# Self-attention of a two-layer decoder: the rows of shifts issued by ACT instead of SP

## The reference

```python
# layer 0: 16 heads of 16, weights are signs times a row mean
q, k, v = split_heads(...)            # B, H, T, Dh
att = softmax(einsum('bhtd,bhsd->bhts', q, k) * scale)
y = einsum('bhts,bhsd->bhtd', att, v)
# layer 1: the same with a mask: 4 heads causal, 12 heads causal within a window of 64
scores = where(mask, -inf, scores)
```

## Time and profile before

| | us |
|---|---|
| median of 3 runs (2166.31 to 2177.34) | 2174.9 |
| the profiled execution | 2166.33 |
| its span, first to last instruction | 2164.6 |

### The profile page before, as it was taken

How to read it: one execution, slowest core, us unless ns; L and a number is a source line. 1 busy time by engine, 2 the same in 40 slices (tenths; PEclk the granted TensorE clock), 3 DMA queues, 4 the chain that set the end, 5 groups by cost and what they waited for, 6 DMA issues and landing times. The chain is left out here.

```text
span 2164.6 us, 35976 instructions
## 1 busy us (share of the span) xinstructions
PE 1685.7 (78%) x12334; PEld 860.6 (40%) x12350; DVE 1328.2 (61%) x3655; ACT 1111.9 (51%) x1526; POOL 929.9 (43%) x955
## 2 busy tenths in 40 slices
PE   4888888888687885577777775677658788999992
PEld 2222222222255563233333333344334455666661
DVE  2767777775177995356666663445267774555554
ACT  2367676765365894245555543355344443444440
POOL 3145455531458522367777764345223341222220
PEclk9899999997698998679999977889879999999996
DMA  4342233320130000334333301422123232222217
GB/s 101 64 70 55 56 49 63 57 45 2 43 83 1 1 1 11 62 58 58 57 56 52 51 11 25 95 52 52 26 90 120 103 132 67 61 62 62 61 49 245
DMA packets 120452, 130.26 MB, mean 60 GB/s; under 512 B 21981, under 2 KB 106973, under 8 KB 120125
## 3 DMA queue, kind: packets, MB, share of 16 engines
q1 hardware_dynamic: 109572, 105.54, 24.0%
q0 software_dynamic: 6480, 18.23, 2.2%
q10 hardware_dynamic: 4224, 4.19, 0.6%
HBM read 79.25 MB, written 47.55 MB: 59 GB/s over the span
## 5 line engine op out<-in xcount | busy, mean ns | idle before, releaser
L653 ACT ACTIVATE at_pexp<-ps 128x1024 f32<-128x1024 f32 (+3 forms) x480 | 385.7, 826 | 185.5 <-PE ps L890 184.5
L714 DVE TENSOR_REDUCE at_mx<-ps 128x1 f32<-128x512 f32 x512 | 323.7, 683 | 137.3 <-PE ps L897 135.5
L897 PE MATMUL ps<-at_ks,at_qs 48*128 48x512 f16 (+3 forms) x1024 | 284.5, 353 | 98.4 <-DVE at_mx L714 41.7
L161 PE MATMUL ps<-mo_wall,mo_xt 128*128 x1704 | 301.8, 327 | 0.9 <-issue 0.9
L890 PE MATMUL ps<-at_qs,at_ks 50*128 50x512 f16 (+4 forms) x1024 | 251.8, 345 | 20.5 <-DMA at_qs<-at_mhl 14.5
L950 PE MATMUL ps<-at_pexp,at_vaug 128*32 128x512 f32 (+4 forms) x2048 | 223.1, 528 | 12.0 <-issue 11.8
L161 PEld LDWEIGHTS ps<-mo_wall,mo_xt 128*128 128x128 f16 x1704 | 161.2, 98 | 94.7 <-issue 4.0
L2258 POOL DMA_INDIRECT mo_yd<-mo_xn,mo_idu x71 | 68.2, 960 | 272.1 <-DVE mo_xn L2520 263.0
L716 DVE CUSTOM_DVE_ANT_0 at_junk<-ps,at_lmask 128x192 bf16<-128x192 f32 x384 | 115.6, 352 | 81.8 <-PE ps L897 80.5
L897 PEld LDWEIGHTS ps<-at_ks,at_qs 48*128 48x128 f16 x1024 | 75.8, 97 | 210.5 <-DVE at_mx L714 121.4
L2311 ACT ACTIVATE mo_sg<-ps 128x512 f32<-128x512 f32 x71 | 42.4, 597 | 194.8 <-PE ps L161 194.8
(11 more groups left out here) (399 smaller groups left out, 3754.8 us busy)
## 6 DMA issues: line engine op xcount, KB each, us to landing
at_qs<-at_scratch SPq DMA_DIRECT2D x96, 128.0 KB, 7.1
at_ks<-at_scratch SPq DMA_DIRECT2D x96, 128.0 KB, 7.7
mo_xr<-mo_xs SPq DMA_DIRECT2D x71, 136.0 KB, 2.4
at_scratch<-at_qkh SPq DMA_DIRECT2D x64, 128.0 KB, 1.8
at_scratch<-at_qkl SPq DMA_DIRECT2D x64, 128.0 KB, 1.8
x_qs<-x_queries SPq DMA_DIRECT2D x48, 128.0 KB
mo_stage<-in_m_gate SPq DMA_DIRECT2D x9, 512.0 KB
mo_stage<-in_m_up SPq DMA_DIRECT2D x9, 512.0 KB
```

What stands on the lines that cost most here:

```text
L161: last = nc.tensor.matmul(out, lhs, rhs, start=(n == 0), stop=(n == len(terms) - 1))
L653: last = act.activation(columns(pexp[:, U % 2, hh], at, n, stride, width), columns(banks(r, ST[S % 2], 2), at, n, stride, width), ACT.Exp, ...
L714: last = ve.reduce_max(out, score, AX.X)
L897: return nc.tensor.matmul(banks(r, MX[i % 2])[:, piece.at:piece.at + piece.n], qs[rows, (n // 2) % 2, h // 2, piece.idx * P:(piece.idx + 1 ...
```

## The change

The function `rows` moves, with its wait and its four transfers, from SP's program to ACT's. ACT calls it in the step MT, right behind `turned_max`. The wait is on the semaphore that ACT's own copy counts up. Sizes, places, semaphores and all other programs stay.

```diff
-            def rows(n):
-                b, half = n // 2, n % 2
-                sp.wait_ge(mhl_ready, n + 1)
-                for par in range(2):
-                    for q in range(2):
-                        sp.dma_start(qs[64 * par + 48 + q:64 * par + 49 + q, b % 2, half * HALF:(half + 1) * HALF, :],
-                                     mhl[(2 * q + par) * HALF:(2 * q + par + 1) * HALF, n % 2, :]).then_inc(rows_in, 16)
...
             for t in range(START, END):
-                for b, half in due(t, "MT"):
-                    rows(2 * b + half)
                 for b, m in due(t - 1, "QK"):
                     save(b, m)
...
+            def rows(n):
+                b, half = n // 2, n % 2
+                act.wait_ge(mhl_ready, n + 1)
+                for par in range(2):
+                    for q in range(2):
+                        act.dma_start(qs[64 * par + 48 + q:64 * par + 49 + q, b % 2, half * HALF:(half + 1) * HALF, :],
+                                      mhl[(2 * q + par) * HALF:(2 * q + par + 1) * HALF, n % 2, :]).then_inc(rows_in, 16)
...
                 for b, half in due(t, "MT"):
                     turned_max(2 * b + half)
+                    rows(2 * b + half)
```

## The result

The changed kernel takes 2202.1 us (median of 4 runs, 2195.8 to 2205.8), the kernel before 2174.2 in 4 runs beside it: ratio 1.0115, 95% interval [1.0079, 1.0152], about 25 us slower. In a later comparison the ratio was 1.0124 [1.0090, 1.0158]. The prediction was 2187.6 (2173 to 2203).

What follows compares the result with a forecast made beforehand. TensorE was busy 78% of the span, with the rows' landing on the path in layer 1. Terms 9.5 + 3.5 + 1.0 + 0.7 = 14.7 us, added to the mean 2172.9, gave 2187.6 us, range 2173 to 2203.

Steps and rivals of the forecast that it cites:

- likeliest account: Whole kernel: ACT's hold delays its next work, +11 to +19 us, likeliest time 2187.6; chance 0.55.
- dear issue: Rival, ACT's queue: at 0.8 us per issue, ACT is held longer and rows land later, 2209; chance 0.12.
- The issue on ACT: ACT behind each copy: four issues at SP's 0.61 spacing, holding it 2.45 us with the wait.
- rival of a cheap issue: ACT's queue: issues below 0.27 us land rows sooner and make the kernel faster, down to 2160; chance 0.08.
- SP gains nothing; the rows land when they did: SP's lost waits and issues are worth nothing; rows land at the same time, the 13.3 us stand stays.
- Layer 0: Layer 0's self-attention: even places 5 x 0.2 = 1.0 us, odd places 7 x 0.1 = 0.7 us more.
- Even places of layer 1: Step 18: late evictions L636, L637 delay the output product by 0.58 at six places, 3.5 us.
- Odd places of layer 1: Step 9: turned_x and y's transposes 1.58 later, 0.17 hidden; 6 x 1.41 + 1.05 = 9.5 us.
- The rival of absorption: Unfollowed slack such as VectorE's mask wins back delays: +10 or less, about 2179; chance 0.25 together with no effect.
- The rival that nothing is felt at all: Waits on the rows hide all of ACT's hold: 2173; chance 0.25 together with absorption.

Runs made afterwards that it cites:

- later comparison: The changed kernel once more, unchanged, against the kernel before: ratio 1.0124.
- experiments 4 and 5: 4: SP sends the rows as before, ACT four idle transfers besides, ratio 1.0167; 5: SP sends two rows, ACT two, 1.0016; both against the kernel before.
- layer-0 kernel: Against the kernel before, ACT issues the rows in layer 0's self-attention alone, layer 1 keeps SP: ratio 1.0014.
- Experiment 1: Against the kernel before, ACT sends only some copies' rows: layer 0 1.0014, layer 1 1.0093, odd of layer 1 1.0092, even of layer 1 1.0024.
- Experiment 3: Changed kernel plus eight unread matrix products on TensorE before layer 1's first transposes of y: ratio 1.0106 to the kernel before.
- odd-only kernel: Against the kernel before, ACT issues the rows of only the odd copies of layer 1: ratio 1.0092.
- even-only kernel: Against the kernel before, ACT issues the rows of only the even copies of layer 1: ratio 1.0024.

## Why the prediction was right, and where it was too small

**The time.** Its likeliest account had a range of its own, 2181 to 2194, and 2202.1 lies above that. The stated range went up to 2203 only to take in part of a dear issue, and the issue was not dear. That the time still lies inside, by 1 us, is luck: another term filled the gap, one that the prediction did not have.

**The issue on ACT.** Taken at 0.61 spacing and 2.45 held. Measured: 2.41 for four, the exponentials behind it after 2.49 of idle. Right. Between the copy's end and the first issue lie 0.03. The rival of a cheap issue, the one on the other side, fell with it, and so did the one of a dear issue: the median is 580 ns and the longest of 128 1177. By the Trainium skill, page "DMA: Bandwidth & Descriptors", section "Anatomy of one DMA — SWDGE (gpsimd) path", a dispatch is some 50 ns; that is the other path, and the trace has 580 here. The Trainium skill's page "Perfetto Trace Analysis", section "DMA Instruction — HWDGE (DVE, Sync)", has the generator locked to one sequencer at a time. If each issue waited for the whole one of the other queue, two each would take up to 2.4 us and four each up to 4.9 (estimates from 0.61 for one); experiments 4 and 5 have 1.20 and 1.36, and 2.50 and 2.87.

**SP gains nothing; the rows land when they did.** Right: the stand at an even place is 1.62 both times.

**Layer 0.** 1.7 us expected; the layer-0 kernel measured +3 us with an interval from -2 to +8. It agrees, without being a test of it. In the changed kernel's trace two steady copies of one kind lie 59.8 or 60.0 us apart and before 59.6, where 0.1 to 0.3 more was said.

**Even places of layer 1.** Expected 0.58 through L636, L637 and the output product. The product is late by 0.51, and waits 0.43 for the eviction, so the path is right. I then took the chain behind it to be late by no more than that. It is late by 0.76, since the mask of VectorE, which is not late itself, now runs beside POOL's split and takes 1.71 for 0.95. No experiment isolates this; it is read from the timeline. The term is 4.5 in place of 3.5 us.

**Odd places of layer 1: the step that was mis-sized.** The prediction put "6 x 1.41 + 1.05 = 9.5 us". The seven waits of L874 for the turned x are there, 2.64 each, and the transposes are 1.53 late where 1.58 was said. But each place costs 2.66. At n = 7 the 0.17 that I took off for the rows is not won: the transposes at half clock take 1.08 for 0.93, and the scores come 1.69 late. The rest, 0.96, comes behind that: after the stand TensorE is at half for some 13 us on end, and the products and scores that open the next chain run in it.

Experiment 1 separates the two parts. Where the clock is at half for as long as before (10.3 us), a place costs 1.3 to 1.5 us: the 1.41 of the prediction was right as the price of the hold. Where it is at half for 3.3 us more, as at every steady place of the changed kernel, it costs 2.66, some 1.2 more. The prediction computed a stand as a delay and nothing else, so this second part stood in it at nothing. The mean granted clock of 0.893 was in the profile, and I never asked where it was low. Experiment 3 agrees from the other side: with the stand filled, transposes and scores go back to full speed and the interval loses 1.4. What the kernel would gain by that stays open, because half clock appears elsewhere.

With 2.66 the term is 18.6 and the sum 18.6 + 4.5 + 1.7 = 24.8 us, beside 25 by the first comparison and 27 by the later one. That it meets the first so closely is partly chance: the 1.7 of layer 0 is not measured, and the last odd place is not like the others. By ratio the odd places alone cost 20 us (16 to 24), though in that kernel's profile the period grew by only 2.1: there the clock was at half for longer at three of the six places only. What decides whether it is stays open.

**The rival of absorption** named VectorE's mask as the place where the delay might be won back. It does win back 0.43 there at n = 7, and more than that is lost to the clock. TensorE also waits less for the maxima than before, 30.1 us in 43 waits for 36.0 in 48 (860 to 1330 us), but the period grows all the same. The rival that nothing is felt at all is refuted by the seven waits.

## What to carry over

An issue holds its engine, here for 0.6 us each, and the page counts that as idle: move issues only to where the engine's idle ahead of its next result that someone waits for is longer than all of them together. Look first at how many issues there are; two instead of four took the cost of sending them by ACT from about 25 us to what cannot be told from nothing. And price a new stand of TensorE with the granted clock of the work behind it, read in windows of a few us at that place, not only with its length.

## What was not expected of the hardware

- With the same work, the same hold and the same stand of 2.64 us, the clock behind an odd copy is at half for 10.4 us at one place and 13.6 at another. The price of the 3 us more of half clock differs by place: 0.7 to 1.3 us behind the odd copies of the odd-only kernel, 0.5 with two issues on ACT, 1.5 behind the even copies.
- The half clock moves rather than goes. Eight idle products took it from behind the odd stand (odd-to-even 27.16 to 25.7) and put it some 20 us behind the even copies (even-to-odd 27.46 to 28.96), and the time did not change. In the even-only kernel it came there at two places of five, with the same work at all five. What decides it is open.
- Two hardware queues that issue together cost each other little: 1.20 and 1.36 us for two issues each, against 1.2 alone. With both queues busy the longest single issue on ACT was 1.49 us, the median 0.72.
- A transfer of two rows is issued in 616 ns, one of one row in 573.
